# Loading the first heads' stacks under the second batch's projections, in memory shared with the feed-forward half

## The reference

```python
def _L0_attn_ref(x, Wq, bq, Wk, bk, Wv, bv, Wo, bo):      # 16 heads of 16
    q = _rope(proj(Wq, bq)); k = _rope(proj(Wk, bk)); v = proj(Wv, bv)
    scores = jnp.einsum('bhtd,bhsd->bhts', q, k) / sqrt(D)
    attn = jax.nn.softmax(scores, axis=-1)
    out = jnp.einsum('bhts,bhsd->bhtd', attn, v)
    ...
    return jnp.einsum('btc,oc->bto', out, Wo) + bo

x = x + _layernorm(_L0_attn_ref(_layernorm(x), ...))
x = x + _layernorm(_L0_ffn_ref(_layernorm(x), ...))       # 2 layers
```

## Time and profile before

| | |
|---|---|
| median of 3 runs | 2952.65 us (2952.53 to 2959.49) |
| profiled execution, its own time | 2961.71 us |
| its span | 2959.7 us |
| PE busy | 2797.1 us (95%) |
| DVE busy | 2320.3 us (78%) |
| ACT busy | 2116.6 us (72%) |
| POOL busy | 972.5 us (33%) |
| mean granted TensorE clock | 0.965 of full |

### The profile page before, as it was taken

How to read it: one execution, slowest core, us unless ns; L and a number is a source line. 1 busy time by engine, 2 the same in 40 slices (tenths; PEclk the granted TensorE clock), 3 DMA queues, 4 the chain that set the end, 5 groups by cost and what they waited for, 6 DMA issues and landing times. The chain is left out here.

```text
span 2959.7 us, 59044 instructions
## 1 busy us (share of the span) xinstructions
PE 2797.1 (95%) x22548; PEld 1742.8 (59%) x22548; DVE 2320.3 (78%) x4282; ACT 2116.6 (72%) x4556; POOL 972.5 (33%) x1145
## 2 busy tenths in 40 slices
PE   7689999999999999999976799999999999999997
PEld 7543333333333333333335688888888788888886
DVE  6559999999999999899905577777777677777774
ACT  5458888888888888788854466666666666667664
POOL 6510000010001000000007455555555465665563
PEclk9859999999999999899988799999999999999999
DMA  5612333334343343334212000000000100000000
GB/s 161 173 27 31 59 54 56 53 66 73 61 71 58 62 72 59 57 50 71 41 53 102 3 5 4 5 5 4 5 5 32 54 11 19 19 11 19 19 18 25
DMA packets 84328, 131.32 MB, mean 44 GB/s; under 512 B 32912, under 2 KB 58960, under 8 KB 76240
## 3 DMA queue, kind: packets, MB, share of 16 engines
q1 hardware_dynamic: 77760, 120.41, 20.9%
q10 hardware_dynamic: 6288, 7.14, 0.7%
HBM read 83.98 MB, written 34.60 MB: 40 GB/s over the span
## 5 line engine op out<-in xcount | busy, mean ns | idle before, releaser
L634 ACT ACTIVATE probs<-scores 128x512 f32<-128x512 f32 x2048 | 1114.9, 596 | 203.2 <-PE scores L565 80.8
L667 DVE TENSOR_REDUCE mx<-aux 128x1 f32<-128x1024 f32 x982 | 1201.1, 1223 | 65.7 <-PE aux L533 58.5
L533 PE MATMUL aux<-k_stack,q_stack 48*128 48x512 f32 x2006 | 760.8, 455 | 15.5 <-DVE mx L675 10.5
L565 PE MATMUL scores<-q_stack,k_stack 50*128 50x512 f32 x2048 | 764.6, 452 | 0.0
L578 PE MATMUL pv<-probs,v_ones 128*32 128x256 f32 x8192 | 661.0, 395 | 0.1
L565 PEld LDWEIGHTS scores<-q_stack,k_stack 50*128 50x128 f32 x2048 | 311.1, 186 | 431.1 <-ACT probs L634 413.6
L578 PEld LDWEIGHTS pv<-probs,v_ones 128*32 128x32 f32 x8192 | 161.9, 108 | 362.7 <-ACT probs L634 291.0
L533 PEld LDWEIGHTS aux<-k_stack,q_stack 48*128 48x128 f32 x2006 | 307.9, 189 | 47.0 <-DVE mx L675 21.0
L484 POOL CAST m_parts<-head_max 128x16 fp32r<-128x16 f32 x32 | 6.3, 198 | 933.7 <-DVE head_max L660 933.7
L1399 ACT ACTIVATE VO<-VO,wo_bo_sb 128x256 f32<-128x256 f32 (+1 forms) x512 | 250.9, 491 | 47.3 <-DVE wo_bo_sb L1523 47.0
L1523 DVE CUSTOM_DVE_ANT_0 VO<-bank,mask_sb,wo_bo_sb 128x256 f32<-128x256 f32 (+1 forms) x512 | 216.2, 469 | 56.2 <-PE bank L1229 56.2
(11 more groups left out here) (172 smaller groups left out, 4706.5 us busy)
## 6 DMA issues: line engine op xcount, KB each, us to landing
q_stack<-qk_dram SPq DMA_DIRECT2D x192, 128.0 KB, 5.3
k_stack<-qk_dram SPq DMA_DIRECT2D x192, 128.0 KB, 7.0
qk_dram<-qkT_hi SPq DMA_DIRECT2D x32, 256.0 KB, 3.1
qk_dram<-qkT_lo SPq DMA_DIRECT2D x32, 256.0 KB, 3.6
VO<-o_stage SPq DMA_DIRECT2D x128, 32.0 KB, 7.0
q_minus_first<-sums_dram SPq DMA_DIRECT2D x32, 128.0 KB, 3.0
w_parts<-tables SPq DMA_DIRECT2D x16, 256.0 KB, 2.5
x_in<-x_dram SPq DMA_DIRECT2D x16, 256.0 KB, 3.2
```

What stands on the lines that cost most here:

```text
L533: return nc.tensor.matmul(out, q_stack[max_rows, n % BODY, tile * P:(tile + 1) * P], k_stack[max_rows, n % BODY, keys * 512:(keys + 1) * 512],
L565: last = nc.tensor.matmul(out, k_stack[0:SCORE_ROWS, n % BODY, s * P:(s + 1) * P], q_stack[0:SCORE_ROWS, n % BODY, j * 512:(j + 1) * 512], ...
L634: nc.scalar.activation(probs[:, e % PROBS], scores[:, item_of_exp(e) % BANKS1], ACT.Exp, scale=float(D1) ** -0.5).then_inc(act_emptied, 1)
L667: nc.vector.tensor_reduce(mx[:, n % BODY, tile, half:half + 1], aux[:, unit % 2].rearrange("p a k -> p (a k)"), AX.X, ALU.max).then_inc(dv ...
```

## The change

- The stacks and `q_minus_first` become objects of a new class `Stacks`, which exists from before the projections to the end. SP loads head 0 behind the stores of the fifth group of tiles and head 1 behind those of the sixth, the rows for scores first, once the first batch's stores have landed (all heads of batch 0 need only those).
- POOL writes the minus ones before its loop over tiles, and negates in five pieces inside that loop, at steps 26, 28, 30, 32 and 33.
- SP no longer waits for its last stores at the end of `project_phase`; it does so in the attention phase, before `load_rows(0)`.
- To make room: the raw projection weights lie in `VO`, `qk_rot` is `qk_cos` (in place, so the next use waits for the transposes), `excess` lies in the last four of the twelve slots of `probs` (one wait more at the ninth exponential), `x1_sb` is a ring of 16 tiles (two waits more per pair from the ninth on), and in the feed-forward half w1, the second layer's qkv weights, the transposed inputs, b2 and others lie in the stacks' memory. b2 is copied within DRAM first and loaded from there.

```diff
+Q_MINUS_PIECES = ((0, 0, 4), (0, 4, 8), (0, 8, 12), (0, 12, TB), (1, 0, LEAD))
+class Stacks:
+    def __init__(self, nc, ctx, qk_dram):
...
+    def load(self, sp, n, row0, loaded):
+        for stack, what, parts in ((self.q, 0, (0, 1, 0)), (self.k, 1, (0, 0, 1))):
+            for i, part in enumerate(parts):
+                sp.dma_start(stack[row0 + i * D1:row0 + (i + 1) * D1, n % BODY, :].bitcast(F32), self.qk_dram[what, part, n]).then_inc(loaded[n % BODY], 16)
...
 # project_phase
+        w_sb = VO[:, 0, 0:NC * 3 * C].rearrange("p (k n) -> p k n", k=NC)
-        qk_rot = sb("qk_rot0", [P, 2, 2 * C])
+        qk_rot = qk_cos
+        NEGATED_AT = (26, 28, 30, 32, 33)
...
-            for g in range(2):
-                sp.wait_ge(stored[g], 16 * STORES * (NT // GROUP // 2))
+                if g == TB // GROUP:
+                    for parity in range(2):
+                        sp.wait_ge(stored[parity], 16 * STORES * (TB // GROUP // 2))
+                if g in (TB // GROUP, TB // GROUP + 1):
+                    n = g - TB // GROUP
+                    sp.wait_ge(stacks.minus_ones_made, n + 1)
+                    stacks.load(sp, n, 0, stacks.for_scores_loaded)
+                    stacks.load(sp, n, SECOND, stacks.for_max_loaded)
...
                     if t >= 2:
-                        dve.wait_ge(rot_done, t - 1)
+                        dve.wait_ge(qkT_in_psum, t - 1)
...
+            for n in range(BODY):
+                nc.gpsimd.memset(stacks.k[SECOND // 2:SECOND, n].bitcast(F32), -1.0).then_inc(stacks.minus_ones_made, 1)
+                pool.wait_ge(stacks.minus_ones_made, n + 1)
+            def negate(i):
+                n, start, stop = Q_MINUS_PIECES[i]
+                rows = slice(0, SPLIT_ROWS)
+                pool.wait_ge(stacks.for_scores_loaded[n], 16 * LOADS)
+                nc.gpsimd.tensor_scalar(stacks.q_minus[rows, n * TB + start:n * TB + stop], stacks.q[rows, n, start * P:stop * P].rearrange("p (t c) -> p t c", c=P).bitcast(F32),
+                                        -1.0, None, ALU.mult).then_inc(stacks.q_minus_made, 1)
+                pool.wait_ge(stacks.q_minus_made, i + 1)
...
                     last.then_inc(sin_done, 1)
+                if t in NEGATED_AT:
+                    negate(NEGATED_AT.index(t))
...
 # attention_phase
+        excess = probs[:, PROBS - BLOCKS:].rearrange("p (i k) c -> p i k c", i=2)
...
-            load(0, SECOND, for_max_loaded)
-            for n in range(2):
-                sp.wait_ge(minus_ones_made, n + 1)
-                load(n, 0, for_scores_loaded)
-                if n == 0:
-                    load(1, SECOND, for_max_loaded)
+            for parity in range(2):
+                sp.wait_ge(qkT_stored[parity], 16 * STORES * (NT // GROUP // 2))
             load_rows(0)
...
+                if e == PROBS - BLOCKS:
+                    act.wait_ge(dve_emptied, unit_of[(OPENING - 1) * BLOCKS] + 1)
...
 # output_phase
+                    if 2 * v >= RING:
+                        pool.wait_ge(x1_stored[(2 * v - RING) // 8], 16)
+                        pool.wait_ge(x1_normed, 2 * v + 2 - RING)
...
 # Weights, feed_forward_phase
+        eng.dma_start(self.b2_dram, ins["b2"]).then_inc(self.b2_copied, 16)
+        eng.wait_ge(self.b2_copied, 16)
+        eng.dma_start(self.b2, self.b2_dram.partition_broadcast(P)).then_inc(self.small_loaded, 16)
...
+        xT_hi, xT_lo = in_k(4, NC, P + 1), in_k(4, NC, P + 1)
+        hT_hi, hT_lo = in_minus(2, NC, 2 * P), in_minus(2, NC, 2 * P)
```

More of the change, by code:

```diff
@@ L39, with project_phase @@
 QKV_LEAD = 4
-def project_phase(nc, ins, x_sb, VO, qk_dram, ident):
+SPLIT_ROWS = 3 * D1
+SCORE_ROWS = SPLIT_ROWS + 2
+SECOND = P // 2
+BLOCKS = T // 512
+BODY = 3
+VW = 32
+HALF = 256
+STEPS = NH * TB
+LEAD = 5
+OPENING = TB + LEAD
+AHEAD = OPENING * BLOCKS + 1
+FIRST_ROWS = TB + 3
+ROWS_STEP, LARGER_STEP = 13, 11
+PROBS = 3 * BLOCKS
+BANKS1 = 3
+LOADS = 6
+CHUNK = 8
+STORES = 8
+TABLES_HEAD = 27
+LOWEST = -3e38
+Q_MINUS_PIECES = ((0, 0, 4), (0, 4, 8), (0, 8, 12), (0, 12, TB), (1, 0, LEAD))
+class Stacks:
+    def __init__(self, nc, ctx, qk_dram):
+        sb = lambda n, s, d=F32: ctx.enter_context(nc.sbuf_tensor(n, s, d))
+        sem = nc.alloc_semaphore
+        self.qk_dram = qk_dram
+        self.q = sb("q_stack", [P, BODY, T], F32R)
+        self.k = sb("k_stack", [P, BODY, T], F32R)
+        self.q_minus = sb("q_minus_first", [P, OPENING, P], F32R)
+        self.minus_ones_made, self.q_minus_made = sem("minus_ones_made"), sem("q_minus_made")
+        self.for_max_loaded, self.for_scores_loaded = ([sem(f"{name}_loaded{slot}") for slot in range(BODY)] for name in ("for_max", "for_scores"))
+    def load(self, sp, n, row0, loaded):
+        for stack, what, parts in ((self.q, 0, (0, 1, 0)), (self.k, 1, (0, 0, 1))):
+            for i, part in enumerate(parts):
+                sp.dma_start(stack[row0 + i * D1:row0 + (i + 1) * D1, n % BODY, :].bitcast(F32), self.qk_dram[what, part, n]).then_inc(loaded[n % BODY], 16)
+def project_phase(nc, ins, x_sb, VO, qk_dram, ident, stacks, qkT_stored):
     with ExitStack() as ctx:
@@ L82, in project_phase @@
         qkT_in_psum, qkT_rounded, qkT_split = sem("qkT_in_psum"), sem("qkT_rounded"), sem("qkT_split")
-        stored = [sem(f"qkT_stored{g}") for g in range(2)]
-        STORES, LOW_ROW = 8, 32
+        stored = qkT_stored
+        LOW_ROW = 32
         CHUNKS = (slice(0, 1), slice(1, 4), slice(4, TB), slice(TB, NT))
@@ L291, in make_mask, with attention_phase @@
                             base=0, pattern=[[-1, P]], channel_multiplier=1)
-def attention_phase(nc, ins, qk_dram, sums_dram, VO, mask_sb, weights, ident, load_output_weights):
+def attention_phase(nc, ins, sums_dram, VO, mask_sb, weights, ident, load_output_weights, stacks, qkT_stored):
     with ExitStack() as ctx:
@@ L371, in _ @@
         def _(sp):
-            def load(n, row0, loaded):
-                for stack, what, parts in ((q_stack, 0, (0, 1, 0)), (k_stack, 1, (0, 0, 1))):
-                    for i, part in enumerate(parts):
-                        sp.dma_start(stack[row0 + i * D1:row0 + (i + 1) * D1, n % BODY, :].bitcast(F32), qk_dram[what, part, n]).then_inc(loaded[n % BODY], 16)
             def load_rows(n):
@@ L738, in output_phase @@
         psY = ps("psY2", [P, 4, 2, C])
-        x1_stored, half_made = sem("x1_stored"), sem("half2_made")
+        x1_stored, half_made = [sem(f"x1_stored{i}") for i in range(2)], sem("half2_made")
         y_done, y_normed_made, x1_made, x1_normed = sem("y2_done"), sem("y2_normed_made"), sem("x1_made"), sem("x1_normed")
@@ L752, in _ @@
             load_weights(sp)
-            for start, end in zip(STORES, STORES[1:]):
+            for i, (start, end) in enumerate(zip(STORES2, STORES2[1:])):
                 sp.wait_ge(x1_made, end)
-                sp.dma_start(x1_dram[:, 2 * start:2 * end], x1_sb[:, 2 * start:2 * end]).then_inc(x1_stored, 16)
-            sp.wait_ge(x1_stored, 16 * (len(STORES) - 1))
+                sp.dma_start(x1_dram[:, 2 * start:2 * end], x1_sb[:, 2 * start % RING:2 * (end - 1) % RING + 2]).then_inc(x1_stored[i % 2], 16)
+            for parity, stores in enumerate((3, 2)):
+                sp.wait_ge(x1_stored[parity], 16 * stores)
         @block.gpsimd
@@ L936, in load_second_wqkv, with feed_forward_phase @@
         eng.dma_start(place[:].bitcast(F32), self.wqkv_parts[part]).then_inc(self.wqkv1_loaded, 16)
-def feed_forward_phase(nc, ins, weights, x_sb, free_space, spare, x1_dram, mask_sb, ident, out):
+def feed_forward_phase(nc, ins, weights, stacks, x_sb, free_space, spare, x1_dram, mask_sb, ident, out):
     with ExitStack() as ctx:
@@ L956, in buffers_in @@
             return take
-        weights.place_second(ctx)
+        in_k = buffers_in(stacks.k[:].rearrange("p b t -> p (b t)"))
+        weights.place_second(in_k)
         wqkv_hi, wqkv_lo, (w1_hi, w1_lo), wo_sb, w2_sb = weights.wqkv_hi, weights.wqkv_lo, weights.w1, weights.wo, weights.w2
@@ L978, in feed_forward_phase @@
         qks_swapped = sb("qks_swapped", [P, LAYERS, 2, D2])
-        xT_hi, xT_lo = (sb(f"xT3_{part}", [P, 4, NC, P + 1], F32R) for part in ("hi", "lo"))
+        xT_hi, xT_lo = in_k(4, NC, P + 1), in_k(4, NC, P + 1)
         qT = sb("qT3", [P, 4, P])
@@ L1048, in shift @@
                 sp.dma_start(x_mid[1:P, s, 2], x_mid[0:P - 1, s, 1]).then_inc(shifted[v % 2], 16)
-                above = zeros[0:1, :] if first(v) else x_mid[P - 1:P, (v - 2) % 4, 1]
+                above = zeros if first(v) else x_mid[P - 1:P, (v - 2) % 4, 1]
                 if v < 2:
```

118 lines of the change are left out of this document (45 added, 73 removed).

## The result

The changed kernel takes 2937.10 us, the median of 7 runs (2933.27 to 2943.32). The kernel before, on the same chip, takes 2959.49 us (7 runs, 2952.53 to 2968.01). The ratio is 0.9921, with a 95% interval of 0.9901 to 0.9942: faster by 23 us. The forecast was 2924 (2908 to 2934), so the sign was right and the time lies 3 us above the range. Its profiled execution took 2935.19 us, its span was 2933.4, its mean clock 0.972.

A forecast was written before the change was run, and what follows sets the result against it. TensorE is nearly always busy except the hole between projections and attention, a chain of landing, loads, negation and mx. Border 2.55 us plus 26.1 to the first maximum, taken as 28.5, off 2952.65 gives 2924 us, range 2908 to 2934.

The forecast's parts named there:

- The chain that the hole is made of: Projections to attention: landing, loads, negation, mx, first maximum in sequence; hiding it brings the third maximum 28.55 us earlier.
- Loads and stores in the queue: Projections: loads served in order delay no store's issue; eighth group's copies wait within existing idle; 0, at most 3 us.
- Border: Projections to attention: SyncE leaves at 127.9 without awaiting landings, border takes 0.5 us, attention begins at 128.4.
- Negations: End of projections, GpSimd: first two pieces vanish in gaps; the third delays sine 31, adding 0.55 us to the path.
- In-place rotation, ring of x1, b2 by way of DRAM: Projections, output and feed-forward: their added waits cost nothing; in-place rotation at most 3 us without its cover.
- Minus ones: Ahead of GpSimd's projection loop: three memsets, 5.4 us, end by 8, before ScalarE's need at 10.14; cost nothing.
- the number that the shift was taken from: Whole kernel: base of 2952.65 us, the median of earlier runs, less 28.5 gives 2924; profiled execution took 2961.7.
- Stacks shared with the feed-forward half: Attention stacks' memory reused by the feed-forward half: same loads at the same times, cost nothing.
- The rival: Feed-forward half slowed by shared memory; decides from 0.45 us a tile, at 0.6 the time is 2962; chance 0.02.
- The clock comes back in the opening: Attention opening: early clock rise saves up to 11 us, with main loop up to 19; 14 taken, 2910; chance 0.12.
- A wait moves into the projections: Projections: late landings or SyncE held while issuing; at worst 10 us, 7 taken, 2931; chance 0.13.
- Hidden but nothing gained: Attention opening: loads hidden, but something else, as a late code fetch, holds it; 2952; chance 0.01.

The follow-up runs named there:

- memory_only: Changed kernel with loads, minus ones, three-piece negations and the wait for stores put back; only new memory places and in-place buffers remain: 2962.73 us, ratio 1.0013 to before.
- after_again: The changed kernel, unchanged, timed and profiled once more: 2933.55 us, ratio 0.9911 to the kernel before.
- before_again: The kernel before, unchanged, timed against itself and profiled again: 2958.76 us, ratio 0.9994.
- wait_at_border: Changed kernel with only SyncE's wait for its stores' landing back at the end of the projections: 2941.28 us, ratio 0.9933 to before.
- w1_shifted: Changed kernel with w1 placed 2 KB higher in the q stack's memory: 2932.90 us, ratio 0.9908 to before.
- after_hT_high: Changed kernel with hT in a high buffer of its own, feed-forward rotary tables in q_minus_first instead: 2931.37 us, ratio 0.9915 to before.
- warm_border: Changed kernel plus 76 unread matmuls in the last two projection steps and behind them, keeping TensorE working to the border: 2938.99 us, ratio 0.9921 to before.
- warm_main_twice: Changed kernel plus unread matmuls at the border, through the opening, and two each at four places early in the main loop: 2921.98 us, ratio 0.9880 to before.

## Why the prediction was right and wrong

**Right, by its own steps.**

- *The chain that the hole is made of*: the third maximum came 29.43 us earlier in the first pair of profiles and 27.4 in the second, for 28.55 forecast; memory_only, without the move, keeps the hole.
- *Loads and stores in the queue*: ScalarE's copy of the eighth group was let go by the sixth group's landing at 115.4, for a landing at 114.1 plus a latency, and the wait took the place of the idle time there, as the 0 in the sum says. In after_again the landing came 1.1 us later (wait of 1.86 us, copy at 116.49) and the projections lost some 0.3 us by it, within the bound of 3. The Trainium skill ("DMA: Bandwidth & Descriptors", Queues, rings and completion order) has descriptors of one ring start in ring order; this copy's release, behind the landings of head 0's loads, agrees.
- *Border*: forecast 128.4, fill of mx at 127.28, and 128.86 in after_again. The 1.1 us of the first come mainly from three things. The whole profile ran ahead by 0.43 us at ScalarE's copy at 113.13 (113.56 before), which is scatter. TensorE's last transposes took 0.66 us and not 1.12, since the clock fell only behind them; in after_again they took 1.12. And the border took 0.4 us for 0.5. With an opening that began 0.2 us later behind it than forecast, that is the 0.9 us that the shift is larger here, so these 0.9 us are no gain of the change.
- *Negations*: the third one does hold sine 31. The sine before it began 0.43 us sooner than before (114.52 for 114.95), sine 31 itself at 117.85 for 117.83: 0.45 us of the 0.55. The first two did not vanish in the gaps: from the fifth group's first store to ScalarE's copy at 110.03 it is 22.57 us in both profiles of the changed kernel and 22.23 before, 0.34 us on the path that the sum did not have.
- *Opening's pace*: 1.87 us, and 0.50 in all of it.
- *In-place rotation, ring of x1, b2 by way of DRAM*: memory_only gives them together at nothing that shows up to the feed-forward half (first rows at 194.37, before 194.89).
- *Minus ones*: the three fills now end at 7.72, and ScalarE's first use of tile 0's deviation stands at 10.08 for 10.14 before: nothing.

**Wrong, first: the number that the shift was taken from.** "It stands 9 us above the median of the runs ...; the shift comes off the median too: 2952.65 - 28.5 = 2924." The kernel before has no such low median. In the comparison itself it took 2959.49, on the second chip 2960.53 over 23 runs, and on no chip less than 2956. Two of the three runs shown lay near the lower end of its scatter, and the profiled execution, at 2961.71, was the more typical one. 2959.49 - 28.5 is 2931.0: this step accounts for 7 of the 13 us by which 2924 was missed.

**Wrong, second: "Stacks shared with the feed-forward half ... All nothing."** This term was put at nothing and is some 4 to 6 us. It is +0.096 us a tile in the dense part; for 64 tiles that would be 6.1 us, and the half grew by 6.0 in the first pair of profiles, but by 3.1 in the second, and by 3.6 from median to median of all profiles. The rival asked for 0.45 us a tile before it would decide, and for that it is five times too small; as a term of the sum it was left out of the main case's own range. The sign of being wrong that it gave, a half above 1350 us, would not have told either: kernels with the fast tiles had halves of up to 1352.9. 2931.0 plus 3.6 to 6.1 is 2934.6 to 2937.1, against the 2937.10 measured. That the upper end hits it exactly is luck, since the interval of the ratio alone spans 12 us.

**Not shown to be a cost of the change: the clock after the opening.** The profile after shows the second rows 4.7 us later than they should be. From first to second rows the ten profiles with the old start of the attention (before, before_again, memory_only and the seven with moved buffers) take 43.6 to 54.7 us, and the five with the new one and no fillers (after, after_again, wait_at_border, w1_shifted, after_hT_high) take 42.6 to 50.1. How long the clock stays at 0.50 there differs from one profile to the next with either start. But after_again repeated the 50.0 us of the first profile, as theory B in its expectation said, and so did after_hT_high, while the most frequent value with the old start is 43.6 us; the median is 50.0 against 45.4. So a systematic loss of up to 5 us there is not ruled out by five profiles. By the last heads' rows nothing of it is left: from the first rows to these it is 1279.5 to 1285.4 us with the new start and 1279.8 to 1296.1 with the old one. At 0.48 us lost for each us the low clock there makes up about 11 us of scatter, where the forecast allowed 2 us either way. The 7.3 us gained further on are due to the clock too: from the second rows on before had 20.5 us of low clock, near 1180, after 3.4, near 416: 17 x 0.48 = 8.

**The rivals.** *The clock comes back in the opening* didn't happen by itself. warm_border shows what it is worth: 7.2 us in the opening where up to 11 was forecast, since two tiles take 3.06 us and not 2.6; and nothing in the main loop, since the clock falls there anew. The Trainium skill ("TensorE: Matmul & The Clock Gate", Part 1) says that sustained activity releases the throttle. The trace after disagrees as the one before did, with 36.45 of 37 us busy at 0.50. warm_main_twice shows the other direction, a fall out of 1.00 with TensorE busy for 2.00 of 2 us. *A wait moves into the projections*: the only one for a landing is ScalarE's above, 1.43 us and absorbed in the first profile, 1.86 us and nearly absorbed in the second. wait_at_border is what its worst case would have been, 5.9 to 7.5 us for the 7 taken; its last landing was awaited until about 134.3, where the queue's sum had 138.5, so loads and stores in one queue were through some 4 us sooner than one after the other. *Hidden but nothing gained* is out by both comparisons, 0.9921 (0.9901 to 0.9942) and 0.9911 (0.9879 to 0.9944).

## What to carry to other kernels

A hole in which loads, a negation and a fill wait for each other is worth its whole length once the loads go in front of the last stores, but only with the wait behind these stores moved away too: here it was 6 to 7.5 of some 28 us. Take the base of a forecast from as many executions as there are, and ask whether three of them are typical; here this was a larger error than any term. And memory moved for room is not free by default: read a stage's time per tile in a profile with the move alone, since 0.1 us a tile, 4 to 6 us here, is lost in the scatter of every total.

## What was not expected of the hardware

- The time of a 128x256 matmul in a dense row depends on where its operands lie: 3.41 or 3.54 us for 30 (114 or 118 ns a matmul) against 3.59 (120 ns). In the kernel before it changes with hT's place (fast at 165 KB and above, slow at 157 KB and below), not with moves of 2 KB; in the new layout, w1 being 75 KB lower, it stays slow even with hT at 193 KB. Why isn't known.
- The clock, once at 0.50, stays there for 11 to 39 us of dense work after the opening, for a time that varies from one profile to the next of kernels with the same attention. The scatter of the whole goes with the mean clock: the kernel before took 2951.44 us at 0.970 and 2979.28 us at 0.960. The clock can also be kept at 1.00 through an opening that otherwise runs wholly at 0.50, by matmuls in the gap ahead of it.
